# A Mamba-2 mixer with an MLP behind it: longer runs of projections on TensorE, and the opening's rows normalised batch by batch

## The reference

```python
x = hidden_states                                  # (2, 1024, 512)
proj = layernorm(x) @ W_in * mup_vector            # 512 -> 1024 (z) + 1024 + 128 + 128 (xBC) + 64 (dt)
z, xBC, dt = split(proj)
xBC = silu(conv_b + sum(conv_w[:, k] * shifted(xBC, k) for k in range(4)))
x_, B, C = split(xBC)                              # 64 heads of 16; B and C of 128
dt = softplus(dt + dt_bias); dA = exp(dt * -exp(A_log))
state = state * dA + (dt * x_) outer B             # per time step
y = state @ C + D * x_
g = y * silu(z); g = g * rsqrt(mean(g * g) + eps) * norm_w
x = x + g @ W_out
h = layernorm(x)                                   # MLP, 512 -> 1408 -> 512, ternary weights with scales
x = x + ((silu((h @ gate_w.T) * gate_s) * ((h @ up_w.T) * up_s)) @ down_w.T) * down_s
```

## Time and profile before

| what | us |
|---|---|
| median of 3 executions | 776.48 |
| lowest and highest | 776.4 and 781.58 |
| the profiled execution's own time | 774.75 |
| its span, first to last instruction | 773.0 |
| PE, DVE, ACT, POOL busy | 742.7, 518.6, 492.7, 294.0 |
| mean granted TensorE clock | 0.985 |

### The profile page before, as it was taken

The page is one execution under the profiler, slowest core; times in us unless marked ns, Lnnn a source line. Parts: engine busy times, 40 slices in busy tenths (PEclk is TensorE's granted clock), DMA queues, the critical chain, the costliest instruction groups (busy, mean ns, idle before and its releaser), DMA issues.

```text
span 773.0 us, 20312 instructions
## 1 busy us (share of the span) xinstructions
PE 742.7 (96%) x8486; PEld 612.8 (79%) x8486; DVE 518.6 (67%) x845; ACT 492.7 (64%) x933; POOL 294.0 (38%) x235
## 2 busy tenths in 40 slices
PE   4887999999999999999999999889999999999998
PEld 4866888788887887887888887678888888888887
DVE  6968976886887797797797698763633532632331
ACT  6989978978978977978888888634312321321330
POOL 2173285366456536627708718540010011002002
PEclk9978999999999999999999999989999999999999
DMA  9823244484475266365376377855113003003002
GB/s 298 236 67 109 55 95 111 96 243 127 83 213 169 80 148 214 99 148 188 93 204 190 83 200 234 230 159 164 55 56 109 0 28 136 0 14 93 3 1 84
DMA packets 42300, 94.97 MB, mean 123 GB/s; under 512 B 9889, under 2 KB 15777, under 8 KB 42017
## 3 DMA queue, kind: packets, MB, share of 16 engines
q1 hardware_dynamic: 42208, 93.67, 42.6%
HBM read 84.73 MB, written 17.57 MB: 132 GB/s over the span
## 4 chain that ended last, share of the span: by engine, by line
PE 61%; DVE 21%; ACT 10%; issue 5%; DMA 2%; SPq 1%; POOL 1%; DVEq 0%; ACTq 0%; POOLq 0%
PE ps_y L1684 10%; PE ps_proj L1671 10%; DVE cx L936 9%; PE ps_out L1671 6%; PE ps_x L1671 6%; PE ps_proj L1223 4%; PE ps_proj L1224 3%; PE ps_proj L1225 3%; PE ps_x L1272 3%; PE ps_y L1295 3%; DVE ring L991 3%; ACT ring L715 2%; PE ps_out L1319 2%; DVE dt_p L911 2%; PE ps_out L1321 2%
## 5 line engine op out<-in xcount | busy, mean ns | idle before, releaser
L530 POOL TENSOR_TENSOR ring<-tokd,ring 128x1024 f32<-128x1024 f32 x64 | 122.5, 1927 | 189.4 <-ACT tokd L710 126.1
L1223 PE MATMUL ps_proj<-xn_hi,win_x_hi 128*128 128x256 f32 x352 | 104.7, 297 | 1.6 <-DVE xn_lo L905 1.6
L1224 PE MATMUL ps_proj<-xn_lo,win_x_hi 128*128 128x256 f32 x352 | 100.2, 285 | 0.0
L1225 PE MATMUL ps_proj<-xn_hi,win_x_lo 128*128 128x256 f32 x352 | 99.9, 284 | 0.0
L936 DVE SCALAR_TENSOR_TENSOR cx<-cin,consts,cx 128x256 f32<-128x256 f32 x240 | 96.4, 484 | 0.0
L1540 POOL TENSOR_TENSOR res<-res,hidden 128x512 f32<-128x512 f32 (+1 forms) x16 | 20.1, 1257 | 166.3 <-DVE hidden L1603 160.7
L1223 PEld LDWEIGHTS ps_proj<-xn_hi,win_x_hi 128*128 128x128 f32 x352 | 67.6, 192 | 14.8 <-issue 11.5
L991 DVE TENSOR_TENSOR ring<-ring,ps_tok 128x1024 f32<-128x1024 f32 x64 | 75.6, 1215 | 4.7 <-ACT ring L719 4.7
L1223 PE MATMUL ps_proj<-xn_hi,win_z_hi 128*128 128x256 f32 x256 | 74.4, 291 | 0.0
L715 ACT ACTIVATE ring<-ring 128x1024 f32<-128x1024 f32 x64 | 66.8, 1060 | 10.2 <-POOL ring L530 10.2
L1224 PE MATMUL ps_proj<-xn_lo,win_z_hi 128*128 128x256 f32 x256 | 72.5, 283 | 0.0
(11 more groups left out here) (186 smaller groups left out, 1889.6 us busy)
## 6 DMA issues: line engine op xcount, KB each, us to landing
ring<-cum_dram SPq DMA_DIRECT2D x128, 256.0 KB, 5.0
xin<-x SPq DMA_DIRECT2D x8, 512.0 KB, 3.9
res<-x SPq DMA_DIRECT2D x32, 128.0 KB, 2.7
x_dram<-res SPq DMA_DIRECT2D x32, 128.0 KB, 3.1
res<-x_dram SPq DMA_DIRECT2D x16, 256.0 KB, 2.7
out<-res SPq DMA_DIRECT2D x15, 256.0 KB, 2.1
x_in_sb<-x_dram SPq DMA_DIRECT2D x3, 1024.0 KB, 5.6
gate_w_copy<-gate_w SPq DMA_DIRECT2D x4, 704.0 KB, 5.9
```

Source lines behind the costliest of these rows:

```text
L530: pool.tensor_tensor(ring[:, g, :, :], own, ring[:, g, :, :], ALU.subtract).then_inc(diffed, 1)
L1223: pe.matmul(out, hi[:, k, :], xn_hi[:, k, :], start=(k == 0), stop=False)
L1224: pe.matmul(out, hi[:, k, :], xn_lo[:, k, :], start=False, stop=False)
L1225: made = pe.matmul(out, lo[:, k, :], xn_hi[:, k, :], start=False, stop=(k == KT - 1))
```

## The change

In the bodies, PE's list takes the projections of the next block in longer runs: P0 and P1 together after the second half of the output projection, P2 and P3 together after `carry`, P4 and P5 together ahead of the first half, and the groups in pairs. `turn_xn` moves behind groups 2 and 3. ACT's list puts `norm_hi` and `keep_tok` behind the clamps of the next step, and `evacuate(i + 1, 0)` behind `gate_hi`; DVE's list puts `norm_lo` behind `gate`, and `mask_cb` and `make_xpad` ahead of `gate_lo`, the update of the state ahead of `normalise`. Other lists hold for the first block. In the opening, x is loaded, measured and normalised one batch after the other, DVE takes three of the four first differences from POOL, `weight_hi(9)` and `weight_lo(9)` move into the body, and PE runs 20 and 6 transposes of `eye` into a free bank before and after the first `turn_xn`. What is computed stays the same.

```diff
-            sp.dma_start(xin[:], x_by_block[0]).then_inc(x_in, 16)
+            sp.dma_start(xin[:, 0, :], x_by_block[0, :, 0, :]).then_inc(x_first, 16)
+            sp.dma_start(xin[:, 1, :], x_by_block[0, :, 1, :]).then_inc(x_in, 16)
...
+            def opening_scale(b):
+                pool.wait_ge(moments_made, b + 1)
+                pool.tensor_tensor(spread[:, b:b + 1], moments[:, b, 1:2], eps[:, b:b + 1], ALU.add).then_inc(eps_added, 1)
+                pool.wait_ge(eps_added, b + 1)
+                pool.tensor_tensor(rstd[:, b:b + 1], spread[:, b:b + 1], minus_half[:, b:b + 1], ALU.pow).then_inc(rstd_made, 1)
+
+            opening_scale(0)
+            opening_scale(1)
...
-            pool.wait_ge(tap_made, N_TAPS)
-            for g in range(GROUPS):
-                diff(0, 0, g)
+            pool.wait_ge(diffed, GROUPS - 1)
+            diff(0, 0, GROUPS - 1)
             body(0, True, False)
...
-                clamp(c, 0)
-                clamp(c, 1)
-                if not first:
+                if first:
+                    keep_tok(c)
+                    clamp(c, 0)
+                    fade(c, 0)
+                    clamp(c, 1)
+                else:
+                    clamp(c, 0)
+                    clamp(c, 1)
                     square(c - 1)
                     evacuate(i, 7)
-                keep_tok(c)
-                fade(c, 0)
-                clamp(c, 2)
+                    keep_tok(c)
+                    fade(c, 0)
+                    clamp(c, 2)
                 fade(c, 1)
+                if first:
+                    weight_hi(9)
+                    clamp(c, 2)
+                    fade(c, 2)
                 clamp(c, 3)
-                fade(c, 2)
+                if not first:
+                    fade(c, 2)
                 fade(c, 3)
                 if first:
                     weight_hi(EVENTS)
                 else:
                     make_skip(i, 0)
-                evacuate(i, 8)
+                if first:
+                    evacuate(i, 8)
                 keep_tokd(i, 1)
+                if not first:
+                    evacuate(i, 8)
                 evacuate(i, 9)
                 if first:
                     weight_hi(EVENTS + 1)
-                if not last:
                     norm_hi(i + 1, 0)
                     norm_hi(i + 1, 1)
-                if first:
                     for n in range(EVENTS + 2, PIECES):
                         weight_hi(n)
                     act.wait_ge(lo_made, LANDED_SKIP)
...
                     mean_square(c - 1, 1)
                 clamp(c + 1, 0)
                 clamp(c + 1, 1)
-                if not last:
+                if not (first or last):
+                    norm_hi(i + 1, 0)
+                    norm_hi(i + 1, 1)
+                if first:
                     evacuate(i + 1, 0)
-                gate_hi(c)
+                    gate_hi(c)
+                    keep_tok(c + 1)
+                else:
+                    keep_tok(c + 1)
+                    gate_hi(c)
+                    if not last:
+                        evacuate(i + 1, 0)
 
                 c = STEPS * i + 1
-                keep_tok(c)
                 fade(c, 0)
...
+                clamp(c, 3)
+                fade(c, 2)
                 if not last:
                     evacuate(i + 1, 2)
...
             weight_hi(0)
-            weight_hi(1)
             norm_hi(0, 0)
             norm_hi(0, 1)
-            for n in range(2, 6):
+            for n in range(1, 6):
...
+            def opening_stats(b):
+                dve.wait_ge(x_in if b else x_first, 16)
+                dve.bn_stats(stats[:, b, :], xin[:, b, :]).then_inc(stats_made, 1)
+                dve.wait_ge(stats_made, b + 1)
+                dve.bn_aggr(moments[:, b, :], stats[:, b, :]).then_inc(moments_made, 1)
+            def opening_normalise(b):
+                dve.wait_ge(rstd_made, b + 1)
+                dve.tensor_scalar(xin[:, b, :], xin[:, b, :], moments[:, b, 0:1], rstd[:, b:b + 1],
+                                  ALU.subtract, ALU.mult).then_inc(xn_made, 1)
+            def opening_diff(g):
+                dve.wait_ge(ring_in[g], 32)
+                dve.wait_ge(tokd_kept, 1)
+                own = tokd[:, 0, CUM, g * GH:(g + 1) * GH].unsqueeze(2).to_broadcast([P, GH, Q])
+                dve.tensor_tensor(ring[:, g, :, :], own, ring[:, g, :, :], ALU.subtract).then_inc(diffed, 1)
...
                 mask_cb(c)
                 make_xpad(i, 0)
-                if first:
-                    weight_lo(9)
-                else:
+                if not first:
                     make_x1(c - 2)
                 mix(c, 0)
                 if not first:
                     scale_carry(i, 0)
-                for g in range(1, GROUPS):
-                    mix(c, g)
-                if not last:
-                    norm_stats(i + 1)
-                    normalise(i + 1)
+                mix(c, 1)
                 if first:
-                    weight_lo(EVENTS)
+                    weight_lo(9)
+                mix(c, 2)
+                mix(c, 3)
+                if first:
+                    update_state(c, 0)
                 if last:
                     mlp_stats(0)
-                update_state(c, 0)
+                else:
+                    norm_stats(i + 1)
+                if first:
+                    normalise(i + 1)
+                    weight_lo(EVENTS)
+                else:
+                    update_state(c, 0)
                 if last:
                     mlp_normalise(0)
                     mlp_normalise(1)
+                elif not first:
+                    normalise(i + 1)
                 if first:
                     weight_lo(EVENTS + 1)
-                if not last:
                     norm_lo(i + 1, 0)
                     norm_lo(i + 1, 1)
                 update_state(c, 1)
...
                         weight_lo(n)
                 make_y(c)
                 gate(i, 0)
+                if not (first or last):
+                    norm_lo(i + 1, 0)
+                    norm_lo(i + 1, 1)
...
+                mask_cb(c)
+                make_xpad(i, 1)
                 gate_lo(c - 1)
+                if not first:
+                    make_x1(c - 2)
                 for n in range(1, 4):
                     soft(i + 1, n)
-                mask_cb(c)
-                make_xpad(i, 1)
-                if not first:
-                    make_x1(c - 2)
                 mix(c, 0)
...
-            norm_stats(0)
+            opening_stats(0)
+            opening_stats(1)
+            opening_normalise(0)
+            opening_normalise(1)
             weight_lo(0)
-            normalise(0)
-            weight_lo(1)
             norm_lo(0, 0)
             norm_lo(0, 1)
-            for n in range(2, 6):
+            for n in range(1, 6):
                 weight_lo(n)
...
+            opening_diff(0)
             weight_lo(8)
+            opening_diff(1)
+            opening_diff(2)
...
+            def keep_warm(n):
+                for _ in range(n):
+                    pe.transpose(ps_out[:, 0:P], eye[:], eye[:])
...
                 project(i, 9)
-                group(c, 2)
-                if not last:
+                if first:
+                    group(c, 2)
                     turn_xn(i + 1, 0)
                     turn_xn(i + 1, 1)
-                if not first:
+                    update(c, 1)
+                    group(c, 3)
+                else:
                     sum_squares(c - 1)
-                update(c, 1)
-                group(c, 3)
-                if not last:
-                    project(i + 1, 0)
+                    update(c, 1)
+                    group(c, 2)
+                    group(c, 3)
+                    if not last:
+                        turn_xn(i + 1, 0)
+                        turn_xn(i + 1, 1)
+                turn_tok(i, 1)
+                turn_x(i, 1)
                 if not first:
                     project_out(c - 1, SECOND_HALF)
-
-                c = STEPS * i + 1
-                turn_tok(i, 1)
-                if not last:
-                    project(i + 1, 1)
-                turn_x(i, 1)
                 if last:
                     mlp_turn(0)
                     mlp_turn(1)
-                if not last:
-                    project(i + 1, 2)
+                else:
+                    project(i + 1, 0)
+                    project(i + 1, 1)
+
+                c = STEPS * i + 1
                 carry(i, 1)
                 if last:
                     project_out(c - 1, FIRST_HALF)
-                if not last:
-                    project(i + 1, 3)
-                add_carry(c)
-                if last:
+                    add_carry(c)
                     for g in range(GROUPS):
                         group(c, g)
                     sum_squares(c - 1)
                     project_out(c - 1, SECOND_HALF)
                     return
```

(26 more changed lines are left out.)

12 lines of the change are left out of this document (5 added, 7 removed).

## The result

The changed kernel took 802.09 us (median of 4 runs, 799.29 to 803.61), the kernel before 777.5 beside it. The ratio is 1.0319, 95% interval 1.0276 to 1.0361: slower by 25 us, outside the range of 771 to 788. The profiled execution took 799.29 (span 797.6), against 774.75 (773.0): 24.6 us of span to explain.

A forecast was written before the change was run, and what follows sets the result against it. PE and a loop from VectorE to ScalarE to VectorE to PE were taken as level bounds. Terms of +4.2, +1.5 and +1.3 gave +7.0 on 774.75, so 781.75, and 783 for the median; range 771 to 788.

The forecast's parts named there:

- Term 1: Middle blocks: longer projection runs and joined groups mean fewer switches on PE, -1.2 us of PE's work per block.
- Term 2: Middle blocks: later P0 delays ScalarE's queue and the last mix, so the period grows 0.7 us, 4.2 over six.
- term 3: Middle blocks: norm_hi behind the clamps lets ring part 1's transfer delay P0, +1.5 us in all, bounds 0 to 3.
- Term 4: Opening and start of block 1: earlier x and P0 against later g_lo and P0 of block 1, +1.3 us.
- g_lo step: Opening: g_lo behind mask_cb and make_xpad makes square wait for 1.4 us of VectorE work, 1.1 of it showing.
- The transposes: Opening: the 26 warm-up transposes could give back 1.7 us of PE, but ScalarE's wait for weight piece 5 takes it: 0.
- second loop: Middle blocks: the path from VectorE to ScalarE to VectorE to PE takes as long as PE's own work, period 60.7 us.
- The last block: Last block: only its second carry comes 0.9 us sooner, the transfers behind it end later: 0 in total.
- C: Rival: ring part 1's transfer decides in most blocks, 786 us for three blocks, 790 for six; chance 0.15 beyond 786.
- A: Rival: PE is the bound after all, so fewer switches pay and the time falls to 766 to 769 us; chance 0.13.
- B: Rival: effects cancel in the middle blocks, last mix stays at 33.5 and the transfer costs nothing, 776 to 778; chance 0.17.
- D: Rival: nothing measurable in middle blocks, the opening alone gains because the clock stays up, 773 us; chance 0.10.

The follow-up runs named there:

- e_pool: The changed kernel without its 26 warm-up transposes, with POOL making xw and fading the state before folding the squares in each block's second step: 789.28 us, ratio 1.0171.
- e_nowarm: The changed kernel without its 26 warm-up transposes and nothing else changed: 789.97 us, ratio 1.0184 to the kernel before.

## Why the prediction was wrong, by its own steps

**Term 1** held. PE's work fell by 1.0 us per period (60.42 to 59.41), forecast 1.2, and went into waits: 1.54 at the carry that ends block 3's period, 1.24 at `update(c+1, 1)`.

**Term 2, +0.7 per middle block,** failed in its sentence that "behind the last mix VectorE has the same 20.1 us of work". Everything up to it was right: second carry at 23.6, P0's end at 20.8, last mix at 34.15 to 34.2 in blocks 1 and 3. Then POOL's fade, 2.4 us later, held the softplus by 0.86 in every block. 0.71 + 0.86 = 1.57 gives 62.2, and 62.17 and 62.18 were measured. Six blocks: 9.4 instead of 4.2. Before's own block 4 had shown it: the rows of that block that I read for term 3 are from the block in which the softplus took 0.85. I had followed three engines and their queues and not the fourth, whose wait for the squares I could have carried along in the same way; that its instruction blocks VectorE's without any semaphore between them is what `e_pool` shows. The wait of `update(c+1, 1)` was inside the slack as I said: the carry behind it still waited for `xpad`.

**Term 3, +1.5,** was right in kind, wrong in its base. The transfer decided in block 2 (P0's evacuation 1.4 late), block 5 (0.8), and by 0.1 to 0.2 in two more: 2.5 of lateness, 1.1 of it in the periods of the five blocks without the large gap. But before had such blocks too: its block 4, which I took as the pattern of a cost to come, was already at 61.38, and with block 1 (61.12, with a gap of 0.61 for instructions) before's five stand 1.5 above its shortest period. Against before, the term came to about nothing. My bounds did not agree either: three blocks like block 4 are 3 times 1.4, so 4.2 and not 3.

**Term 4, +1.3,** measured +3.4. The g_lo step that I priced at 1.1 was one of two limits; the other, P2 behind a carry that waits 4.6 us, I had only looked for in the middle blocks. Both together gave 2.2 behind the carry, and it is open why the carry came 2.3 later with them.

**The transposes, 0,** failed most. I had their gain taken by "ScalarE's wait for piece 5", which is true of the opening to 0.01 us, and gave them no price. Their price is that they shift the fetches: 9.7 us in the old kernel, 9 to 12 in the changed one. That is as much as the second loop's loss, and it belongs to no term of my sum: I had taken instructions on an idle engine to be free.

**The last block, 0,** measured -1.2 up to the second carry and +5.6 behind it: 2.0 is the longer gap (3.99 against 1.95), 1.1 the wait for x1 (2.98 against 1.86), 1.6 the second phase, the remaining 0.9 is probably half clock behind these waits. The 1.6 of the second phase (256.5 to 258.0, from its first transpose) stays open: it also came and went between kernels with the same phase (256.5 in `e_nowarm`, 258.7 in `e_pool`).

Of the rivals, C had the side but not the mechanism; the conditions of A, B and D never arose. By runs, the 25 us are roughly: transposes 10, blocks' order 12 (9.4 of it the second loop), block 0's order the remaining 3. The parts do not add up exactly, since each shifts the fetches of the others: measured twice, the transposes gave 9.7 and 9 to 12, and the blocks' order 11.7 and 14.8.

## What to carry to other kernels

When a profile shows idle time by "issue" in the middle of identical instructions, count the engine's instructions up to it and look for instruction packets among the DMA: a kernel like this one, of 17000 instructions on TensorE, can lose 10 us to 26 harmless transposes put far ahead, and two versions should not be compared to 1% without looking at where those gaps fell. Count in the trace and not in the source: my 102 fillers were 204 matmuls. Small matmuls use up instructions fastest (256 in 1.4 us), so I would keep runs of them away from the moments at which large transfers start; no run here tried that. And if a step is moved, follow every engine it delays to that engine's next large instruction, and ask which engine that one locks out.

## What was not expected of the hardware

- TensorE stops for its instructions: 39 gaps of 1.3 to 5.2 us, all at 193 above a multiple of 256 of its instructions, each ending 0.9 to 1.7 us after a 16 KB packet landed.
- Idle time cost twice: behind the gap of 5.02 us the granted clock was 0.50, and twelve matmuls took 2.4 us more.
- The warm-up transposes did raise the clock: the granted clock was 1.00 from 6.52 us on, without them from 13.05. Without them P0 began at the 1.2 GHz level, with them at 2.4 GHz; PE in `e_nowarm`, then in the changed kernel:

```profile
10.40 0.41 PE L1287 MATMUL ps_proj<-xn_hi,win_x_lo 128*128 128x256 f32 x1
10.61 0.41 PE L1285 MATMUL ps_proj<-xn_hi,win_x_hi 128*128 128x256 f32 x1
```

```profile
9.66 0.28 PE L1287 MATMUL ps_proj<-xn_hi,win_x_lo 128*128 128x256 f32 x1
9.78 0.28 PE L1285 MATMUL ps_proj<-xn_hi,win_x_hi 128*128 128x256 f32 x1
```

Steps of 0.21 against 0.12. The Trainium skill ("TensorE: Matmul & The Clock Gate", Part 4) has it that a transpose in transpose mode does not count. Whether these fp32 transposes ran in that mode the trace does not tell, it lists them as plain matmuls; counted they did. The gain was lost in the next wait: P2 began at 16.96 with them and 17.58 without, and the second carry of block 0 at 75.20 and 75.19.
- A plain f32 matmul of 64 x 32 by 64 columns appears as two pairs of weight load and matmul: 204 for 102. All in one place of the array they took 11.5 us at 2.4 GHz and 21.8 at 1.2 GHz; spread over eight places, the first 189 took 2.1.
